# Weighted sums for two key tiles in every second step of the attention rounds, instead of one tile in almost every step

## The reference

```python
x = x + _L0_xattn_ref(_layernorm(x), ctx_1024, ctx_1024, Wq, Wk, Wv, Wo)
x = x + _L0_attn_ref(...)      # a mix over heads and token blocks
x = x + _L0_ffn_ref(...)       # one of 8 experts
x = x + _L1_xattn_ref(_layernorm(x), ctx_1024, ctx_1024, ...)
x = x + _L1_attn_ref(...)      # a linear scan over the tokens, gelu, norm
x = x + _L1_ffn_ref(...)       # two of 8 experts, three linear layers

# each cross attention
scores = jnp.einsum('bhqd,bhkd->bhqk', qh, kh) * scale
attn = jax.nn.softmax(scores, axis=-1)
out = jnp.einsum('bhqk,bhkd->bhqd', attn, vh)
```

## Time and profile before

| | |
|---|---|
| time, median of 3 runs | 1041.88 us (1038.27 to 1042.79) |
| the profiled execution | 1040.78 us |
| its span (first to last instruction) | 1039.0 us |
| TensorE matmuls busy | 950.1 us, 91% |
| TensorE weight loads busy | 627.0 us, 60% |
| VectorE busy | 628.6 us, 61% |
| ScalarE busy | 549.3 us, 53% |
| GpSimd busy | 200.6 us, 19% |
| mean granted TensorE clock | 0.985 |

### The profile page before, as it was taken

One profiled execution on the slowest core, in us unless ns is written; L12 is line 12 of the kernel. 1 busy time (PEld: TensorE's weight loads), 2 busy tenths in 40 slices (PEclk: granted clock), 3 DMA queues, 4 the chain that ended last, 5 costly groups with the idle time before them and its releaser, 6 DMA issues.

```text
span 1039.0 us, 35578 instructions
## 1 busy us (share of the span) xinstructions
PE 950.1 (91%) x15476; PEld 627.0 (60%) x15476; DVE 628.6 (61%) x1047; ACT 549.3 (53%) x1035; POOL 200.6 (19%) x232
## 2 busy tenths in 40 slices
PE   4868889999899999999998899898798899999998
PEld 2436565656566665666655566566678544445887
DVE  5746666667575665857667676774774665345332
ACT  4548776676667667556666456656634521212200
POOL 4302112121111212111121111411446210000000
PEclk9989999999999999999999999999899999999999
DMA  8686376553634452354334335224211323223100
GB/s 278 165 284 210 99 212 161 154 169 83 190 96 143 122 138 63 110 138 118 100 111 117 98 103 141 55 61 165 84 49 69 129 81 122 81 88 116 42 1 21
DMA packets 70513, 123.78 MB, mean 119 GB/s; under 512 B 34468, under 2 KB 45764, under 8 KB 67096
## 3 DMA queue, kind: packets, MB, share of 16 engines
q1 hardware_dynamic: 69528, 119.84, 39.1%
q0 software_dynamic: 544, 1.34, 0.4%
q10 hardware_dynamic: 288, 0.33, 0.1%
HBM read 64.81 MB, written 17.31 MB: 79 GB/s over the span
## 4 chain that ended last, share of the span: by engine, by line
PE 69%; DVE 13%; ACT 8%; issue 5%; DMA 3%; SPq 1%; POOL 1%; ACTq 0%; DVEq 0%; POOLq 0%
PE ps L693 67%; DVE mpart L1334 4%; ACT p L1099 3%; DVE rinv L1351 1%; SPq L458 1%; DMA stage<-in_wkv 1%; ACT ch L1057 1%; DMA c32b<-in_ctxT 1%; PE ps L832 1%; DVE cl L1309 1%; ACT kh L1074 1%; ACT k L1073 1%; DVE wl L1365 1%; PE ps L862 1%; DMA stage<-in_fw 1%
## 5 line engine op out<-in xcount | busy, mean ns | idle before, releaser
L1334 DVE TENSOR_REDUCE mpart<-ps 128x2 f32<-128x800 f32 (+1 forms) x256 | 252.5, 988 | 129.2 <-PE ps L693 128.2
L1099 ACT ACTIVATE p<-ps 128x512 f32<-128x512 f32 (+1 forms) x416 | 225.5, 595 | 186.7 <-PE ps L693 185.2
L623 POOL TENSOR_TENSOR kl<-k,kh 128x400 f16<-128x400 f32 (+1 forms) x128 | 117.7, 920 | 468.3 <-ACT kh L1074 468.3
L693 PE MATMUL ps<-p,v 128*17 128x64 f32 x6656 | 132.4, 222 | 0.6 <-issue 0.6
L693 PEld LDWEIGHTS ps<-p,v 128*17 128x17 f32 x6656 | 98.6, 98 | 38.4 <-issue 36.3
L693 PE MATMUL ps<-wvh,ch 128*128 128x256 f16 (+1 forms) x416 | 115.6, 278 | 1.5 <-issue 1.5
L693 PE MATMUL ps<-wvh,cl 128*128 128x256 f16 (+1 forms) x416 | 115.0, 276 | 0.0
L693 PE MATMUL ps<-wvl,ch 128*128 128x256 f16 (+1 forms) x416 | 114.9, 276 | 0.0
L693 PE MATMUL ps<-xch,wh 128*128 128x512 f16 (+2 forms) x384 | 113.8, 310 | 0.0
L693 PE MATMUL ps<-kh,qbcur 64*128 64x400 f16 (+1 forms) x512 | 86.8, 337 | 29.4 <-DVE mpart L1334 26.1
L693 PE MATMUL ps<-xcl,wh 128*128 128x512 f16 (+2 forms) x384 | 113.7, 310 | 0.0
(11 more groups left out here) (206 smaller groups left out, 1462.8 us busy)
## 6 DMA issues: line engine op xcount, KB each, us to landing
ks<-kh SPq DMA_DIRECT2D x256, 100.1 KB
w<-in_wgu SPq DMA_DIRECT2D x16, 1024.0 KB, 4.8
ks<-kl SPq DMA_DIRECT2D x128, 100.1 KB
w<-in_wd SPq DMA_DIRECT2D x8, 1024.0 KB, 4.8
c32a<-in_ctxT SPq DMA_DIRECT2D x16, 400.5 KB, 5.3
cparts<-ch SPq DMA_DIRECT2D x8, 800.5 KB, 6.9
cparts<-cl SPq DMA_DIRECT2D x8, 800.5 KB, 9.0
c32a<-in_ctxT SPq DMA_DIRECT2D x12, 400.0 KB, 3.2
```

Source lines behind the costliest of these rows:

```text
L623: nc.gpsimd.tensor_tensor(kl[:, mt, k0:k0 + w], k32[:, ku % 2, 0:w], kh[:, mt, k0:k0 + w], ALU.subtract).then_inc(sem("klo_done"), 1)
L693: return nc.tensor.matmul(o, lhsT, rhs, start=start, stop=stop, skip_group_check=shared)
L1099: nc.scalar.activation(p32[0:n, step % PRING, BANK * side:BANK * side + BANK], ps[0:n, side, :], ACT.Exp, scale=DH ** -0.5).then_inc(sem(" ...
L1334: nc.vector.reduce_max(mpart[:, j0:j0 + 3:2, quarter], o.rearrange("p (b c) -> p b c", b=2)[:, :, 0:w], AX.X).then_inc(sem("max_done"), 1)
```

## The change

The W of a step now takes two tiles, in the steps 5, 7, 9 and 11 (tiles k-3 and k-2), as it did already in step 3; the steps 1, 4, 6, 8, 10 and 12 have none; and step 0 takes the tiles 10, 11 and 12 of the round before.

```diff
 STEP_UNITS = {0: ["V2", "S", "P0", "W"],
-              1: ["V3", "S", "P1", "W"],
+              1: ["V3", "S", "P1"],
               2: ["V4", "P2", "V5", "S", "P3"],
               3: ["W", "S", "P4"],
-              4: ["K4", "S", "P5", "W", "O"],
+              4: ["K4", "S", "P5", "O"],
               5: ["V6", "P6", "K5", "S", "P7", "W"],
-              6: ["K6", "S", "P8", "W"],
+              6: ["K6", "S", "P8"],
               7: ["K7", "S", "P9", "W"],
-              8: ["V0", "P10", "V1", "S", "P11", "W"],
+              8: ["V0", "P10", "V1", "S", "P11"],
               9: ["N0", "S", "P12", "W"],
-              10: ["N1", "S", "P13", "W"],
+              10: ["N1", "S", "P13"],
               11: ["N2", "S", "P14", "W"],
-              12: ["S", "P15", "N3", "W", "T"]}
-
-WEIGH_AT = {0: (11,), 1: (12,), 3: (0, 1), **{k: (k - 2,) for k in range(4, KT)}}
+              12: ["S", "P15", "N3", "T"]}
+
+WEIGH_AT = {0: (10, 11, 12), **{k: (k - 3, k - 2) for k in range(3, KT - 1, 2)}}
...
-                        elif name == "W" and k > 1:
+                        elif name == "W" and k > 0:
                             for kt in WEIGH_AT[k]:
                                 weigh(g, kt)
...
-            for k in range(2):
-                for kt in WEIGH_AT[k]:
-                    weigh(G - 1, kt)
+            for kt in WEIGH_AT[0]:
+                weigh(G - 1, kt)
```

## The result

The changed kernel takes 1055.26 us (median of 4 executions, 1054.89 to 1057.82), the kernel before 1040.61 (4, 1038.27 to 1042.79): 1.0146 of it, 95% interval 1.0116 to 1.0177. It is slower by 14.6 us. I had predicted 1039.0, and the range up to 1046 did not hold it.

The account below looks back on a forecast made before the run. The prediction took the kernel as TensorE-bound (69% of the chain), though not everywhere, with waits swallowing some moves. Its terms summed to -2.9 us, from 1040.78 to 1037.9, given as a median of 1039; range 1031 to 1046.

Parts of the forecast that it names:

- The price in the free stream: TensorE where nothing waits: a W of its own costs 0.57 us, a second tile 0.45, so each merge gains 0.12.
- Step 12 to T: T waits for VectorE's maxima anyway, so removing the W in front of it gives 0 in 15 rounds.
- Steps 0 and 1: Two tiles more in step 0, no W in step 1: +0.33 us a round, +4.6 in sum.
- Step 4: W between P5 and O removed: P7 waits for VectorE and comes only 0.17 us earlier in eight rounds; sum -1.9.
- Steps 5 and 6: A tile added (+0.45) and a W removed (-0.57): 0.12 us gained in 10 rounds, sum -1.2.
- Steps 7 and 8: Step 7's tile is free before P11 in 10 of 15 rounds, +2.2; step 8's W gains 0.57 in all 15, -8.6.
- Steps 9, 10 and 11: Steps 9 and 10 gain 1.6 us over 13 rounds; step 11's added tile is paid in rounds 2 to 9, +3.6.
- The sum, -2.9: All places together: -2.9 us against the profiled execution's 1040.78, so 1037.9; predicted median 1039.
- one row stands for its pattern: Working assumption of the place-by-place pricing: one profile row represents its pattern, with rounds counted from the same timelines.
- some eight rounds classed wrongly at 0.45 each: The margin on the -2.9: give or take 3 to 5 us; this own case had chance 0.6.
- merging pays everywhere: Rival: stalls move along, so the full -11.5 us is gained, 1030; chance of 1036.7 or less 0.22.
- The short steps run into ScalarE: Rival: S of step 9 held 0.57 us each round by V1's copy, sum +5.7, 1046.5; chance 0.17.

Follow-up runs that it names:

- e7: The kernel before with only the W of step 12 taken out, tiles 10 and 11 in step 0, tile 12 in step 1: 1050.07 us, 1.0082.
- e3: The changed kernel's pairs in steps 5, 7, 9 and 11, but the last tiles weighed in steps 12, 0 and 1 as before: 1037.87 us, 0.9968.
- e1: The changed kernel with the large loads aw and wq issued at step 5 instead of step 0 of round 2: 1050.61 us, 1.0096.
- e2: The changed kernel, but rounds 11 and 13 weigh their tiles as in the kernel before: 1051.9 us, 1.0102.
- e9: The changed kernel with the edits of e1 and e2, and the wo load at step 2 of round 9: 1044.91 us, 1.0040.
- e10: e6 with the wo load at step 2 of round 9 instead of step 8 of round 8: 1036.27 us, 0.9964.
- e4: The kernel before with single tiles kept in steps 4 to 11, but none in steps 12 and 1 and three in step 0: 1055.47 us, 1.0140.
- e5: The changed kernel's pairs, but tile 10 in step 12, tiles 11 and 12 in step 0, none in step 1: 1038.38 us, 0.9981.
- e6: e5, but in 11 of 15 rounds tiles 2 and 3 stand singly in steps 4 and 5, pairs from step 7: 1037.03 us, 0.9969.
- e8: The kernel before, W untouched, with the loads aw and wq issued ahead of the query stores in round 2: 1043.38 us, 1.0017.

## Why the prediction was wrong, point by point

- **The price in the free stream**: right. 0.57 for a W that goes, 0.45 for a tile that comes, 1.47 for three tiles are what the steps show. The idle time in front of the weight loads fell by 18.6 us, from 36.3 to 17.7, or 0.20 for each W merged, but TensorE's stream gained 0.12 for each.
- **Step 12 to T, 0**: right. T is 1.94 behind P15 in 12 rounds of 15, as before, and e7 shows it alone. It was W's cover that was given away here, at 0.45 a round. What the term left out is the clock: in step 12 of round 13 the fall behind the longer idle time costs 1.77, where the removal was to give 0.
- **Steps 0 and 1, +4.6**: right, +0.33 in nine rounds and +4.3 over fifteen. The triple W also delays TensorE's program by 0.8 at the moment when that matters, which the term did not see.
- **Step 4, -1.9**: the mechanism (P7 waits for VectorE, so W was cover) was right in seven rounds, where P7 comes as late after P5 as before. It was mis-sized in the even rounds from 8 on: P7 comes 0.88 earlier there (4.72 to 3.84), and with 0.67 and 0.44 in rounds 0 and 2 that is -4.6 instead of -1.9. In round 7, which the rows show, the 0.17 did not come: 4.21 before and after. The kernel waits there for GpSimd, as told below the list. In rounds 11 and 13 the sign is wrong: +1.2 each, by the fall of the clock.
- **Steps 5 and 6, -1.2**: right in size. From P7 to P9 it is -0.12 or so in seven rounds and -1.3 over the thirteen without 11 and 13, which have +0.3 each.
- **Steps 7 and 8, +2.2 and -8.6**: P12 is 0.57 earlier behind P11 in 14 of 15 rounds, at 1.64 where I said (404.25 to 405.89 in round 7): -8.0. But the second tile in step 7 was free in front of P11 in 4 rounds, not 10, and cost 0.45 or so in ten and 0.21 in one (4.8 instead of 2.2). With one more round in which P12 gains nothing, this term forecast 3.2 too much gain. The 2.7 more of step 4, rounds 11 and 13 left aside, made up for most of it, which is luck.
- **Steps 9, 10 and 11**: -0.8 instead of -1.6, and +3.9 instead of +3.6 without round 8's late piece. No wait appeared in front of S.
- **The sum, -2.9**: the ten rounds without a loss that comes once add up to -0.5, where the sum has about -2 for ten. The pairs alone measure -3 (e3); the round's end costs 5 by its pattern.

**What the term of step 4 had left out.** VectorE's product (L1354 before, L1353 after) takes 0.29 us where no `kl` of GpSimd runs already when it starts. Where one does, the product ends 0.15 behind the end of `kl`. In rounds 4, 6, 7 and 9 that holds before and after: the product starts 0.30 earlier, takes that much longer and ends where it did. In the even rounds from 8 on the product now starts just ahead of `kl` and gets through 0.88 sooner. Round 10, before:

```profile
518.29 0.90 POOL L623 TENSOR_TENSOR kl<-k,kh 128x401 f16<-128x401 f32 x1 [9.79 <-ACT kh L1074]
518.46 0.87 DVE L1354 TENSOR_TENSOR oT<-osum,rinv 128x128 f32<-128x128 f32 x1
```

and after:

```profile
528.89 0.29 DVE L1353 TENSOR_TENSOR oT<-osum,rinv 128x128 f32<-128x128 f32 x1
529.02 0.91 POOL L623 TENSOR_TENSOR kl<-k,kh 128x401 f16<-128x401 f32 x1 [10.11 <-ACT kh L1073]
```

The step that failed is the one behind the sum, that "one row stands for its pattern" in all rounds, and its margin of "some eight rounds classed wrongly at 0.45 each". I allowed for wrong classes of one mechanism and for none of another. Of the 14.6 us, e1 takes 4.6 (instructions late behind `aw`, with the half clock that follows), e2 3.4 (rounds 11 and 13, where the fall to half clock in steps 4 and 5 is 2.9 of it in the trace), and e9, which adds the load of `wo` to both, 2.4 more. About 4 remain (3.8 in e9's own comparison, 2.2 to 6.1), of which the 5 of the round's end and the -3 of the pairs give 2. The other 2 are not attributed by a run of their own and lie within that interval; e9's trace has falls of the clock of that size (0.50 and 1.57).

Of the rivals, "merging pays everywhere" was wrong at T and at P7. "The short steps run into ScalarE" had the right sign and, at 1046.5, the nearest time, but for a reason that did not occur: the waits for exponentials fell from 8.2 to 4.8 us.

Open are: why step 11 of round 8 keeps 0.62 us in e10 and none in e9, why the clock falls in one execution and not in another with the same idle times, and part of what e4, e5, e6 and e7 have above their forecasts; in e4 and e7 the falls in step 12 are 3.1 and 2.7 us of it in one trace each.

## What to carry to other kernels

A wait for another engine is cover: work that stands in it is free and should stay there, and a tile moved out of it pays its full price where it lands (0.45 us a round here). That was so for T; for the W of step 4 it was so in some rounds only. When a trace shows an idle time without a releaser between two instructions with the same inputs, look at the instruction queue's packets and at the large loads issued just ahead; with the load moved by a few steps the kernel was 4.6 us faster. And when a change shifts a long program by a fraction of a microsecond, put into the range what comes once: late instructions and stretches at half clock moved this result by some 10 us, while every repeated term was right to 3 or so.

## What the runs showed of the hardware

- TensorE can run out of instructions. Its pieces are packets of 16 KB on a queue of their own; behind a load of 1 MB and one of 256 KB a piece began 6.5 us later than the one ahead of the load in the kernel before (155.25, not 148.77), and TensorE stood still for 4.15 us (3.58 in e8, 4.14 in a second trace, 0.31 with the loads moved).
- The granted clock fell to 1.2 GHz after idle times of 0.69 and 1.74 us with work between them in 10 of 16 cases, and after 0.12 and 1.74 in the same place in none of 16 (once, in e9, 1.3 us later). It fell behind T after a single idle time of 1.9 to 2.1 us in five of five cases (round 13), and of 1.6 in four of seven (round 14). Within one program it fell in three of six cases in three traces, so one trace is no proof against such a cause; the ten timed executions of that program spread over 7 us.
- Such a stretch costs about 1.4 us where TensorE is the bound (0.99 in step 4 and 0.81 to 0.99 in step 5, of which 0.45 is the tile).
- VectorE's product `oT<-osum,rinv`, 128 x 128 in fp32, took 0.29 us by itself, and did not end before GpSimd's `kl` where that had begun first: with 0.83 us of overlap it took 0.98 (round 7 after), with 0.53 it took 0.68 (before).
